# Experts by sorted blocks of tokens instead of all eight experts on every token

## The reference, cut to what matters

```python
def _L1_ffn_ref(x, W_qkv, b_qkv, W_gate, b_gate, W_experts, b_experts):
    NUM_HEADS, TOP_K = 16, 2
    qkv = (x @ W_qkv + b_qkv).reshape(B, S, 3, H, hd)
    q, k, v = qkv[:, :, 0], qkv[:, :, 1], qkv[:, :, 2]
    attn = softmax(einsum('bqhd,bkhd->bhqk', q, k) / sqrt(hd))
    attn_out = einsum('bhqk,bkhd->bqhd', attn, v).reshape(B, S, D)
    gate = softmax(x @ W_gate + b_gate)                  # 8 experts
    top_g, top_i = top_k(gate, TOP_K)
    combine = sum(one_hot(top_i, E) * top_g[..., None], axis=2)
    expert_out = einsum('bsd,edf->bsef', x, W_experts) + b_experts
    moe_out = einsum('bsef,bse->bsf', expert_out, combine)
    return attn_out + moe_out
h = h + _L1_ffn_ref(_layernorm(h), ...)                  # x is the normalized h
```

## Time and profile before

| | us |
|---|---|
| median of 3 runs | 2212.42 (2212.3 to 2214.53) |
| the profiled execution's own time | 2215.91 |
| its span in the profile | 2214.1 |
| quantized layer, 836 to 1130 | 294 |
| experts, 1322 to 1736 | 414 |
| softmax attention, 1736 to 2214 | 478 |

### The profile page before, as it was taken

How to read it: one execution, slowest core, us unless ns; L and a number is a source line. 1 busy time by engine, 2 the same in 40 slices (tenths; PEclk the granted TensorE clock), 3 DMA queues, 4 the chain that set the end, 5 groups by cost and what they waited for, 6 DMA issues and landing times. The chain is left out here.

```text
span 2214.1 us, 36468 instructions
## 1 busy us (share of the span) xinstructions
PE 2060.5 (93%) x11553; PEld 1337.2 (60%) x11553; DVE 1603.9 (72%) x4388; ACT 901.8 (41%) x2108; POOL 737.7 (33%) x1355
## 2 busy tenths in 40 slices
PE   7997989998999998999979849999999999999997
PEld 5886753335888885777743227888888433333332
DVE  3335977774777767999948846767676888888881
ACT  1113655552112214444424411222222167777777
POOL 3553645553333332333311101111111523333332
PEclk9997989998999999999989969999999789999999
DMA  4332769872000000000010001121217213333310
GB/s 131 114 104 53 176 161 201 165 160 64 1 1 1 1 1 15 1 1 1 1 57 9 10 28 39 40 49 39 49 40 169 43 35 78 78 79 78 78 45 20
DMA packets 212523, 133.86 MB, mean 60 GB/s; under 512 B 113370, under 2 KB 201604, under 8 KB 212356
## 3 DMA queue, kind: packets, MB, share of 16 engines
q1 hardware_dynamic: 212356, 131.78, 25.4%
HBM read 89.96 MB, written 41.38 MB: 59 GB/s over the span
## 5 line engine op out<-in xcount | busy, mean ns | idle before, releaser
L2693 DVE TENSOR_REDUCE attend_mx<-ps 128x1 f32<-128x512 f32 x512 | 320.8, 681 | 40.3 <-PE ps L2387 39.2
L2530 ACT ACTIVATE attend_w<-ps 128x512 f32<-128x512 f32 x512 | 280.5, 596 | 92.6 <-PE ps L2401 91.1
L2003 PE MATMUL ps<-keep_early,moe_zT 128*128 128x256 f32 x1056 | 243.5, 384 | 4.4 <-DVE keep_h L2158 4.4
L2003 PEld LDWEIGHTS ps<-keep_early,moe_zT 128*128 128x128 f32 x1056 | 196.5, 191 | 40.0 <-DVE keep_h L2158 15.5
L2387 PE MATMUL ps<-keep_x,keep_o 96*128 96x512 bf16 x512 | 208.0, 411 | 7.2 <-DVE attend_mx L2693 5.3
L2401 PE MATMUL ps<-keep_o,keep_x 99*128 99x512 bf16 x512 | 191.6, 384 | 2.7 <-ACT attend_w L2530 2.7
L2158 DVE SCALAR_TENSOR_TENSOR keep_h<-ps,moe_g,keep_h 128x256 f32<-128x256 f32 x264 | 127.6, 483 | 61.6 <-PE ps L2003 53.7
L2387 PEld LDWEIGHTS ps<-keep_x,keep_o 96*128 96x128 bf16 x512 | 50.1, 98 | 183.3 <-DVE attend_mx L2693 136.1
L1003 DVE SCALAR_TENSOR_TENSOR keep_early<-ps,first_causal 128x512 f32<-128x512 f32 (+3 forms) x256 | 113.7, 484 | 48.0 <-PE ps L885 43.6
L981 POOL TENSOR_TENSOR keep_early<-keep_early,first_causal 128x128 f32<-128x128 f32 x256 | 113.2, 458 | 86.5 <-ACT keep_early L949 85.5
L1216 PE MATMUL ps<-mlp_zT,keep_early 128*128 128x128 f32 x1056 | 129.1, 281 | 8.0 <-ACT mlp_zT L1258 8.0
(11 more groups left out here) (341 smaller groups left out, 4110.0 us busy)
## 6 DMA issues: line engine op xcount, KB each, us to landing
tok_xin<-in_xk SPq DMA_DIRECT2D x64, 256.0 KB, 2.7
qk_parts<-qkv_parts SPq DMA_DIRECT2D x33, 384.0 KB, 3.2
qk_parts<-moe_parts SPq DMA_DIRECT2D x33, 384.0 KB, 3.2
keep_o<-qk_parts SPq DMA_DIRECT2D x16, 384.0 KB, 4.7
keep_x<-qk_parts SPq DMA_DIRECT2D x16, 384.0 KB, 5.8
v_all<-qkv_v SPq DMA_DIRECT2D x33, 136.0 KB, 3.3
v_all<-moe_v SPq DMA_DIRECT2D x33, 136.0 KB, 3.2
keep_early<-v_all SPq DMA_DIRECT2D x16, 272.0 KB, 6.8
```

The lines of the kernel that those rows point to most:

```text
L2003: last = nc.tensor.matmul(ps[:, E0 + pair % 2, e % 2 * D:(e % 2 + 1) * D], zT[:, u, k * P:(k + 1) * P], we[e][:, k, :], start=(k == 0), st ...
L2530: nc.scalar.activation(w[:, j, kt % 2, :], ps[:, SC + (HG * k + j) % RING, :], ACT.Exp)\
L2693: nc.vector.tensor_reduce(mx[:, t, k:k + 1], ps[:, MX + (TB * k + t) % RING, :], AX, ALU.max)\
```

## The change

The eight experts are no longer applied to every tile. Each token's normalized row is written twice to a table in memory, `sorted`, once under each of its two experts; the table has room for 34 x 128 rows per expert, and 73 x 128 spare rows behind. Afterwards the table is worked off in 73 blocks of 128 rows, each of one expert only, and in place: the rows of a block are read, multiplied with that expert's matrix, its bias is added, and the result is written over them. 73 blocks are enough for 2 x 33 tiles of rows plus the unfilled ends of seven experts. The attention pass then fetches the two rows of each token, multiplies them with the two gates and adds them to `env.h`.

In detail:

- `pass_fp4`: DVE sets five tiles of `env.x` to zero, and SP writes them over the whole table, 44,160 rows of 1 KB, in three DMAs.
- `pass_moe`, by tiles: the loop is written out for 33 + 4 steps, each with pieces of several tiles. DVE takes the eight logits, sorts them (MAX), finds their indices (MAX_INDEX) and marks the two chosen experts. PE counts by small bfloat16 matmuls with a triangular matrix how many rows each expert has so far, DVE picks each token's two row numbers from that, and POOL scatters the tile twice with an indirect DMA (`scatter`). The four early loads for the attention are spread over tiles 13 to 25 (`LATE` is 20).
- `pass_moe`, between: thirteen small DVE operations on one partition turn the counts into a list of 73 experts and 73 first rows (`slots`).
- `pass_moe`, by blocks: SP reads the first row into a register (TENSOR_LOAD) and loads the block (three buffers). PE transposes it, DVE copies it out, ACT copies the expert's matrix to a fixed place (its number, too, comes from a register), PE multiplies, DVE adds the bias and POOL stores the block from its own queue (three buffers).
- `pass_attend`: POOL issues two fetches for each of two tiles in every slot, and combines them after its other work with three operations a tile. `add` and the last addition on DVE wait for it.

```diff
@@ pass_fp4, SP and DVE
+            sp.wait_ge(s_blank, 1)
+            runs = io["sorted"].rearrange("(p n c) d -> p n (c d)", p=P, c=BLANK)
+            n = runs.shape[1] // 3
+            zero = env.x[:, 0:BLANK, :].rearrange("p (a c) d -> p a (c d)", a=1)
+            for i in range(3):
+                sp.dma_start(runs[:, i * n:(i + 1) * n, :], zero.to_broadcast([P, n, BLANK * D])).then_inc(env.s_blank_z, 16)
...
+            nc.vector.memset(env.x[:, 0:BLANK, :], 0.0).then_inc(s_blank, 1)
@@ pass_moe
+CAP = (NT + 1) * P
+NSLOT = 2 * NT + E - 1
+ROWS = E * CAP + NSLOT * P
+BLANK = 5
...
+            sp.dma_start(b_rep[:, :, :].rearrange("p e d -> p (e d)"),
+                         io["b_experts"].rearrange("e d -> (e d)").rearrange("(a n) -> a n", a=1).to_broadcast([P, E * D]))\
+                .then_inc(s_in, 16)
...
+            for j in range(NSLOT):
+                row = sp.value_load(slot_row[0:1, j:j + 1], min_val=0, max_val=ROWS - P)
+                past(sp, s_dT, j - NY + 1)
+                sp.dma_start(zs[:, j % NY, :], io["sorted"][bass.ds(row, P), :]).then_inc(s_zs[j % NY], 16)
@@ PE
-            def experts(s, u, pair):
-                past(pe, s_acc, 4 * s + pair - 1)
-                for e in (2 * pair, 2 * pair + 1):
...
+            def expert(j):
+                pe.wait_ge(s_dz, j + 1)
+                pe.wait_ge(s_dW, j + 1)
+                past(pe, s_y, j - 1)
+                for k in range(KD):
+                    last = nc.tensor.matmul(ps[:, D_Y[j % 2], 0:D], zsT[:, j % 2, k * P:(k + 1) * P], w_now[:, j % NW, k, :],
+                                            start=(k == 0), stop=(k == KD - 1))
+                last.then_inc(s_dM, 1)
@@ ACT
+            for j in range(NSLOT):
+                e = act.value_load(slot_e[0:1, j:j + 1], min_val=0, max_val=E - 1)
+                past(act, s_dM, j - NW + 1)
+                nc.scalar.copy(w_now[:, j % NW, :, :].rearrange("p k d -> p (k d)"),
+                               we[:, bass.ds(e, 1), :].rearrange("p a f -> p (a f)")).then_inc(s_dW, 1)
@@ POOL
+            def scatter(s):
+                pool.wait_ge(s_place, s + 1)
+                for j in range(2):
+                    nc.gpsimd.indirect_dma_start(io["sorted"], bass.IndirectOffsetOnAxis(ap=pos[:, s, j:j + 1], axis=0),
+                                                 z[:, s % NZ, :], None).then_inc(s_scat[s % NZ], 16)
+            pool.wait_ge(env.s_blank_z, 48)
...
+            for i in range(NT + 3):
+                if live(i + 2):
+                    deviation(i + 2)
+                if live(i - 3):
+                    third(i - 3)
+                if live(i - 2):
+                    scatter(i - 2)
+            pool.wait_ge(s_slots, 1)
+            for j in range(NSLOT):
+                row = pool.value_load(slot_row[0:1, j:j + 1], min_val=0, max_val=ROWS - P)
+                pool.wait_ge(s_y, j + 1)
+                nc.gpsimd.dma_start(io["sorted"][bass.ds(row, P), :], y[:, j % NY, :]).then_inc(s_yout[j % NY], 16)
@@ DVE
+            def result(j):
+                e = dve.value_load(slot_e[0:1, j:j + 1], min_val=0, max_val=E - 1)
+                dve.wait_ge(s_dM, j + 1)
+                past(dve, s_yout[j % NY], 16 * (j // NY))
+                nc.vector.tensor_tensor(y[:, j % NY, :], ps[:, D_Y[j % 2], 0:D],
+                                        b_rep[:, bass.ds(e, 1), :].rearrange("p a d -> p (a d)"), ALU.add).then_inc(s_y, 1)
@@ pass_attend, POOL
             def add(group, parity, b, g):
                 pool.wait_ge(s_n, group + 1)
+                pool.wait_ge(s_e, TB * (b + 1))
...
+            def fetch(i):
+                s = ORDER[i]
+                past(pool, s_e, i - 3)
+                for j in range(2):
+                    at = 2 * (i % 4) + j
+                    nc.gpsimd.indirect_dma_start(land[:, at, :], None, io["sorted"],
+                                                 bass.IndirectOffsetOnAxis(ap=env.pos[:, s, j:j + 1], axis=0))\
+                        .then_inc(s_land[at], 16)
```

More of the change, by code:

```diff
@@ L1944, in pass_moe @@
-        s_E, s_acc, s_TC, s_cT, s_be, s_beh, c_g = (a.sem(n) for n in ("E", "acc", "TC", "cTs", "be", "beh", "c_g"))
-        s_out, s_vout = a.sems("out", 2), a.sems("vout", 2)
-        block = a.block()
-        GL, LATE = 9, 6
+        lg = a.sb("lg", [P, E])
+        top = a.sb("top", [P, E])
+        below = a.sb("below", [P, 2, E])
+        ex = a.sb("ex", [P, 2, E])
+        total = a.sb("total", [P, 2])
+        which = a.sb("which", [P, E], U32)
+        which_f = a.sb("which_f", [P, 2])
@@ new lines, in pass_moe @@
+        chosen = a.sb("chosen", [P, 3, 2, E], BF16)
+        place = a.sb("place", [P, 2, E])
+        place_f = a.sb("place_f", [P, 2])
+        tri = a.sb("tri", [P, 2, P], BF16)
+        start = a.sb("start", [1, 1, E], BF16)
+        one = a.sb("one", [1, P], BF16)
+        full = a.sb("full", [1, E, NT])
+        blocks = a.sb("blocks", [1, 3, E])
+        order = a.sb("order", [1, E, E])
+        room = env.heads.room
+        after = room.rearrange("p a t -> p (a t)")[0:1, 0:2 * NSLOT * E].rearrange("p (n j e) -> p n j e", n=2, e=E)
@@ L2046, in _ @@
+            turn(0)
+            for j in range(NSLOT):
+                if j + 1 < NSLOT:
+                    turn(j + 1)
+                expert(j)
         @block.scalar
@@ new lines, in _ @@
+            for s in range(2):
+                stats(s)
+                apply(s)
+            for i in range(NT + 4):
+                if live(i - 1):
+                    rank(i - 1)
+                if live(i - 3):
+                    value(i - 3)
+                if live(i - 1):
+                    choose(i - 1)
+                if live(i + 2):
+                    stats(i + 2)
+                if live(i - 1):
+                    weigh(i - 1)
+                if live(i - 2):
+                    places(i - 2)
+                if live(i + 2):
+                    apply(i + 2)
+                if i - 2 == NT - 1:
+                    slots()
+                if live(i - 3):
+                    split(i - 3)
+                    if i - 3 == 0:
+                        keep_class()
+                if i - 4 >= 2:
+                    take_class(i - 5)
@@ L2193 @@
+            take_class(NT - 1)
+            turned(0)
+            for j in range(NSLOT):
+                if j + 1 < NSLOT:
+                    turned(j + 1)
+                result(j)
 UNITS = 2 * B
@@ L2600, in _ @@
                     class_weights(x)
+                owed = [i for i in (2 * x.s, 2 * x.s + 1) if i < NT]
+                for i in owed:
+                    fetch(i)
                 if x.follows():
```

403 lines of the change are left out of this document (262 added, 141 removed).

## The result

The changed kernel took 2280.28 us (median of 4 runs, 2278.83 to 2284.09), the kernel before 2213.31: ratio 1.0305, 95% interval 1.0287 to 1.0323. It is slower by 67 us. I had forecast 2172, in a range of 2105 to 2268, and gave slower a chance of 0.33: wrong in sign and outside the range. Two executions, one of the unchanged kernel (4234 us) and one of the run with the combining held back (3889 us), took far longer than all the others and are left out of the medians.

What follows compares the result with a forecast made beforehand. PE bounds the experts' stage; afterwards a DVE-POOL ring and POOL's blocks. New stage 221 + 5 + 7 + 131 + 4 = 368 for 414: -46, +1 zeroing, +3 attention = -42; forecast 2172 us, range 2105 to 2268.

Steps and rivals of the forecast that it cites:

- What bounds the kernel before: Experts' stage, 414 us: PE sets the 12.14 us a tile, 7.38 of it the experts' matmuls.
- The tile loop: Experts' stage by tiles: bound passes from PE to a DVE-POOL ring, 3.8 + 2X = 6.2 a step; loop 221 us together.
- The early loads: Tile loop: SP's four early loads for the attention stand ahead of stores that ACT waits for, +5 us.
- The half clock: Rival, slower, chance 0.05: PE's pauses lower its granted clock, a block takes 2.7 us, +66, total 2238.
- The blocks: The 73 blocks: POOL is the last engine at 1.8 us a block, 131 us; ends 1.4 and 2.9.
- X: Time for which one DMA holds POOL, in loop and blocks: taken as 1.2 us, turning point 1.5.
- dear descriptors: Rival, slower, chance 0.20: POOL's DMA costs 1.9 us, not 1.2, in loop and blocks; +100, total 2272.
- the rival: Register loads in series, slower, chance 0.11: a load takes 1.39 on all four engines, POOL's block 2.7; +66, 2238.
- The table: Between tiles and blocks: thirteen operations, some 5 us, half beside the closing steps, then SP's first load, about 3: +7.
- The entry: Start of the experts' stage, 11 us: some 5 until the 1 MB of replicated biases has landed.
- The end of the stage: Behind the last block: a last store and the barrier, +4 us.
- The attention: POOL's fetches and combining are covered with 3 us to spare, slot still 27.2; late first slots +3.

Runs made afterwards that it cites:

- fillers: Changed kernel plus eight matmuls a step on PE that nothing reads, placed where PE waits for the copy of class scores: 2217.03 us, 1.0004.
- the copy first: Changed kernel with DVE's copy of the class scores moved from the end to the head of its step, ahead of the ranking: 2165.82 us, 0.9791.
- the scatters stand first: Changed kernel with the copy of class scores at the head of DVE's step and POOL's two scatters ahead of its third part: 2169.93 us, 0.9794.

## Why the prediction was wrong, step by step

**What bounds the kernel before** stood: PE's matmuls.

**The tile loop: the step that failed.** I took what each engine has to do, found one ring (DVE and POOL) and took the longest: 6.2. I didn't go through the other waits that close on themselves. PE's class scores wait for a copy that stands last in DVE's step, behind the split, behind ACT, behind the same step's projection. That order is new. In the kernel before, the copy that a tile's class scores wait for is done a whole step ahead of them, and the split stands behind it:

```profile
1565.24 0.19 DVE L2180 COPY keep_cs<-ps 128x32 f32<-128x32 f32 x1
...
1572.11 0.68 DVE L2136 TENSOR_TENSOR moe_rest<-moe_qkf,moe_parts 128x512 f32<-128x512 f32 x1
...
1575.85 0.19 PEld L2025 LDWEIGHTS ps<-moe_kq,moe_qkf 128*128 128x128 f32 x1
```

The loop written out for 37 steps puts the copy of tile i-5 behind the split of tile i-3, and PE's class scores of tile i-4 behind the projection of tile i-3, so that the ring closes within one step. And the experts' 7.4 us a tile, which stood between projection and class scores and could have covered the 3.2 us of waiting, are gone (no run puts them or the old order back, so their shares stay open). My text says "PE: 4.8", as if PE had no wait inside a tile but the forecast's, and asks nowhere what its class scores wait for. Up to the first block's result the stage took 355.6 us, where loop, early loads and table were to take 233: +123. Of these, 90 had gathered by the last normalization (1610.7); the closing steps, most of them 9.3 to 10.6 us instead of 4.5, and the table added 33. The runs split a step's excess of 4.3: 2.7 go with the clock (fillers, which set the step themselves by then, so the clock's share can be a little larger), all of it with the order.

**The early loads** (+5) show nowhere in the changed kernel's steps; with the copy first three steps took 8.3 to 8.9 instead of 6.08, 8 us in all. **The half clock** had a chance of 0.05 and a price for the blocks only. The blocks were at 0.99 (1677.6 to 1779.1); the loop, at 0.71, was where it struck.

**X**, the time for which a DMA holds POOL, was 1.2. It is 1.0 for a scatter with 0.3 behind it, and 0.54 for a block's plain store, two values where I had one. In the run with the copy first the two scatters take 2.49 us of the ring (1403.22 to 1405.71), where 2X was 2.4, and the rest 3.58, where it was 3.8: 6.07 for 6.2. The port rule that I quoted for *dear descriptors* shows in a few scatters only: one of 2.45 us beside DVE's building of the class token's products (1349.08), and 1.16 beside the normalization where the scatters stand first. **The blocks** were to be bound by POOL at 1.8; X = 0.54 put that aside, and the ring over the store buffers holds: 1.41, 102 us, not 131. That I had this ring at 1.45 is partly luck: with 0.54 in it, its formula gives (0.43 + 0.54 + 2.7) / 3 = 1.22, and what makes up the rest is not shown. (The dear end of a block, 2.9, doesn't come out of its terms either: 1.39 + 0.13 + 1.2 is 2.7, as in the rival.) A register load, taken at 0.5, is 0.27 to 0.73:

```profile
L2182 ACTq TENSOR_LOAD <-moe_slot_e x73: 272/492/733, 1665.7 to 1775.4; - x73
L2360 DVEq TENSOR_LOAD <-moe_slot_e x73: 298/305/631, 1675.8 to 1777.9; - x73
```

On DVE that is half of the floor of about 600 ns for which I quoted the Trainium skill, page "DMA: Bandwidth & Descriptors", section "Latency and other measured facts"; the measurement decides. **The table**: 5.4 us from 1651.36, as forecast, but 4.6 of it, not half, delayed a closing step, whose split had its operand from 1652.2 on. **The entry**: a wait of 4.15 for the biases, as forecast. **The end of the stage**: 12 us from the last block's result to the attention's first work at 1791.1, not 4. POOL waits 10 us of it; what for, beyond the landing of its last stores, no run here separates.

**The quantized layer**: the zeroing is hidden, as forecast; its three DMAs, issued from 836.7 on, had landed by about 950.

**The attention**: the late first slot cost 2.6 for 3. But "both are covered" was wrong, a second step that failed: I compared POOL's work with POOL's gap, and not with what DVE does in that gap. DVE's subtractions lost 0.86 there, and a slot got 0.6 longer. Here the Trainium skill, page "SBUF — State Buffer", section "Terms", has the rule: DVE and GpSimd arbitrate for a port pair whose lock is held for a whole instruction, and the loser is blocked outright. The rows agree (0.32 and 1.18). I had quoted that page for the scatters alone.

Sum: -42 forecast; +123 for the loop, -29 for the blocks, +8 for the end of the stage, +10 for the attention, -1 elsewhere make +69, for 68.3 in the span. The attention's 10 are 9 in its slots and 2 between DVE's last addition and the end of the span (7.9 us, for 5.8 before), which no run explains, less the 0.4 by which the first slot cost less than forecast.

The rival *dear descriptors* gave 2272, near the result, by a mechanism that wasn't there: leaving the scatters out of the changed kernel changed nothing (2283.22 for 2280.28). A number near the result isn't evidence for the cause beside it.

## What to carry to other kernels

Before an engine's longest work is taken away, or the pieces of a loop are put in a new order, go through the waits between engines: follow each backwards through both programs until it closes, and add up the ring without that work. The last operation of an engine's step is the first suspect when another engine waits for it; moving one copy of 0.19 us was worth 114 us. When two engines that share a port get more work at once, compare their timelines against each other, not each with its own gap.

## What was not expected of the hardware

- Some of DVE's operations with source and target in SBUF last until a POOL operation beside them is over, however small they are: 8 columns 1.85 us, 2 columns 1.23, two subtractions 1.18 for 0.32. For the last, two runs show POOL to be the cause: it went when POOL's work was left out and when it was held back. The value's addition, which reads PSUM, stayed at 0.42 in all these rows, and so did the statistics (0.42) and the sorting (0.17) where they lay beside POOL's third part. The Trainium skill, page "VectorE: DVE Perf Modes", section "What auto-detection actually checks", names a single source and a destination in SBUF, with even or equal outermost dimensions, as the condition of the mode 2×_2P, in which an operation uses both of DVE's ports. That fits the subtraction of 8 columns and the cast.
- Matmuls without a reader paid 63 us; the granted clock from 1500 to 1600 rose from 0.71 to 0.97.
- An indirect DMA of 128 rows holds POOL for about 1 us whether it scatters (0.99 at the median of 66, up to 2.45) or fetches (0.96), and 0.3 pass before the next. The fetches:

```profile
L2802 POOL DMA_INDIRECT keep_early<-sorted,keep_early x66: 956/960/1052, 1811.4 to 2244.3; - x66
```
